# Ring tiles of 1024 columns loaded in four transfers (by field and by column half) in place of two (by field)

## The chip, the cores and the metric

The kernel runs on one core of a Trainium2 chip. The metric is the device time of one execution in microseconds (us), taken as the median of several runs. The engines of a core work in parallel and meet only at semaphores: TensorE (PE in the profile, PEld for its weight loads), VectorE (DVE), ScalarE (ACT), GpSimd (POOL), and SyncE (SP), which here does nothing but issue DMA transfers and wait for room. "SPq", "ACTq" and "POOLq" are the instructions of these engines that issue transfers or handle semaphores; they are not counted as busy.

## The reference

A recommendation model (xDeepFM) with a batch of 512, 39 fields and embeddings of 16 numbers:

```python
e = emb_table[feat_index]                       # 512 x 39 x 16
flat = e.reshape(512, -1)
linear_part = flat @ linear_w + linear_b
x0 = e
h1 = relu(einsum('bhd,bmd,ohm->bod', x0, x0, conv_w1) + conv_b1[None, :, None])   # 128 outputs
nxt, hi1 = split(h1, 2, axis=1)                 # 64 and 64
h2 = relu(einsum('bhd,bmd,ohm->bod', nxt, x0, conv_w2) + conv_b2[None, :, None])  # 128 outputs
res = concatenate([hi1, h2], axis=1).sum(axis=2)
y = relu(bn(flat @ deep_w1 + deep_b1, bn_g1, bn_b1))     # 400, batch norm over the batch
y = relu(bn(y @ deep_w2 + deep_b2, bn_g2, bn_b2))        # 400
out = concatenate([linear_part, res, y], axis=1) @ out_w + out_b
```

## The kernel before

The batch is cut into nine parts: parts 0 and 1 have 32 rows each, parts 2 to 8 have 64. One row of the batch gives 16 columns (one for each embedding number), so a tile of parts 0 and 1 has 512 columns and one of parts 2 to 8 has 1024; BANK is 512 columns, and CHUNKS_OF[j] says how many BANKs a tile of part j has (1 or 2).

GpSimd gathers the embeddings row by row, TensorE transposes them, ScalarE copies the result out and writes it to a scratch tensor in HBM, xs, laid out by part and field: for each field of a part one contiguous row of 512 or 1024 numbers of 4 bytes.

Layer 1 multiplies pairs of fields elementwise and contracts them with w1 ("x" tiles, six for each part; the multiplicand is put in place by TensorE at line 878, the product goes to placed). Layer 2 needs, for each pair of fields 2t and 2t+1, the product of the 64 rows nxt with field 2t (partitions 0 to 63) and with field 2t+1 (partitions 64 to 127): 20 tiles for each part. Most of these are "d" tiles: SP loads field 2t, repeated over 64 partitions, and field 2t+1, repeated over the other 64, into one of the eight slots of ring (a source with a partition step of zero); DVE multiplies the slot in place by p_n at line 732; TensorE contracts it with w2 at line 898. The few "p" tiles are put in place by TensorE instead of being loaded. Of the d tiles 38 have 512 columns and 129 have 1024.

The order of all tiles is one list written out by hand, SEQ; LOADED is the list of the d tiles in it, m the number of a tile in LOADED and m % 8 its slot. Each engine walks the same list. TensorE contracts a tile either in full precision (four matmul records for 1024 columns) or, for the tiles in SPLITS, as a high part (made by ScalarE, line 1095) and a low part (made by DVE at line 700 or by GpSimd at line 609), six records.

SP's program: the first loads of indices and weights; then for each m a wait until the slot's former tile has been used up (wait_used, its wait stands at line 372 in the profile), then the transfers of line 572. Behind the first d tile of part 3 (m = 55) stand load_flat for parts 0 and 1 and load_deep, 36 transfers of the deep layers' inputs and weights (lines 505 and 526 to 533), which TensorE needs from line 966 on. Every transfer raises the slot's semaphore s_load by 16, and DVE waits in product for the sum.

Of the kernel before, what the change touches and what calls it, by code (L numbers as in the profile page):

```python
# [6 lines left out]
BATCH, FIELDS, DIM, VOCAB = 512, 39, 16, 125000  # L7
H1, H2 = 128, 128
NEXT = H1 // 2
# [8 lines left out]
BANK = 512  # L18
# [11 lines left out]
TOK_OF = [DIM * r for r in ROWS_OF]  # L30
CHUNKS_OF = [t // BANK for t in TOK_OF]
# [102 lines left out]
RING, PLACED_RING, HIGH_RING, LOW_RING = 8, 4, 6, 7  # L134
# [33 lines left out]
SEQ, AT, WHERE = [], {}, []  # L168
# [13 lines left out]
LOADED = [s for s, tile in enumerate(SEQ) if tile[0] == 'd']  # L182
# [9 lines left out]
def rows_of(s):  # L192

    kind, _, t = SEQ[s]
    return X_ROWS[t] if kind == 'x' else 128
# [6 lines left out]
def build(nc, idx, emb, lin_w, lin_b, w1a, w1b, b1, w2, b2, dw1, db1, g1, be1, dw2, db2, g2, be2,  # L202
# [5 lines left out]
    xs = nc.dram_tensor("xs_scratch", [BLOCKS * FIELDS, TOK], F32).ap()  # L208

    def xs_at(b, field):  # L210

        return FIELDS * DIM * FROM[b] + field * TOK_OF[b]

    def xs_rows(b, field, n, stride):

        return bass.AP(xs.tensor, xs_at(b, field), [[stride * TOK_OF[b], n], [1, TOK_OF[b]]])

    ctx = ExitStack()
    with ctx:
        def sb(name, shape, dt=F32):  # L220
            return ctx.enter_context(nc.sbuf_tensor(name, shape, dt))
# [4 lines left out]
        def sem(name):  # L226
            return ctx.enter_context(nc.semaphore(name))
# [10 lines left out]
        ring = sb("ring", [128, RING, TOK])  # L238
# [93 lines left out]
        s_load = [sem(f"s_load{r}") for r in range(RING)]  # L332
# [36 lines left out]
        def own_wait(eng, semaphore, value):  # L369

            eng.wait_ge(semaphore, value)
            eng.sem_inc(s_past, 1)
# [67 lines left out]
        for b in range(1, PARTS):  # L440
            j, n = WHERE[LAST_X[b]]
# [40 lines left out]
        def scratch_write(eng, b, writes):  # L482

            for q, group, groups, fields in writes:

                r = ROWS_OF[b]
                dst = bass.AP(xs.tensor, xs_at(b, FLAT_FIELDS[b][0] * q + PER_GROUP[b] * group),
                              [[r, DIM * fields], [PER_GROUP[b] * TOK_OF[b], groups], [1, r]])
                src = xT[0:DIM * fields, q, r * group:r * (group + groups)].rearrange("p (g b) -> p g b", g=groups)
                eng.dma_start(dst, src).then_inc(s_xs, 16)  # L490

        def load_first_x(eng, b):
            eng.dma_start(xa[0:FIELDS, b % 2, 0:TOK_OF[b]], xs_rows(b, 0, FIELDS, 1)).then_inc(s_first_x, 16)

        def load_xa(eng, b):
            cols = slice(0, TOK_OF[b])
            for g in range(1, 3):
                eng.dma_start(xa[FIELDS * g:FIELDS * (g + 1), b % 2, cols], xs_rows(b, 0, FIELDS, 1)).then_inc(s_xa, 16)
            eng.dma_start(xa[3 * FIELDS:, b % 2, cols], xs_rows(b, 0, EXTRA, 1)).then_inc(s_xa, 16)
# [7 lines left out]
        def load_half_indices(eng, block, g):  # L507

            r, n = ROWS_OF[0], PER_GROUP[0]
            half, quarter = divmod(g, 2)  # L510
            src = idx[ROWS * half:ROWS * (half + 1), block, n * quarter:n * (quarter + 1)].rearrange("(c r) f -> r c f", c=2)
            eng.dma_start(idx_raw[r * g:r * (g + 1), block, :].rearrange("r (c f) -> r c f", c=2), src).then_inc(s_idx, 16)

        def load_w1(eng, dst, src):

            for t, p, n, (tile, row) in W1_RUNS:
                eng.dma_start(dst[p:p + n, t, :], src[row:row + n, tile, :]).then_inc(s_w, 16)  # L517


        @block.sync  # L520
        def _(sp):
            def load_deep():

                for c, p, first, fields in FLAT_PIECES:
                    row, r = DIM * first, DIM * fields
                    sp.dma_start(dw1_sb[p:p + r, c, 0:HIDDEN], dw1[row:row + r, :]).then_inc(s_small, 16)
                    sp.dma_start(dw1_sb[p:p + r, c, HIDDEN:], lin_w[row:row + r, :]).then_inc(s_small, 16)
                for n, v in enumerate((db1, g1, be1, db2, g2, be2)):
                    sp.dma_start(vec[:, n, :], v).then_inc(s_small, 16)
                for dst, src in ((lb_sb[HID_K:, :], lin_b), (ow_y_sb[HID_K:, HID_T - 1:], ow_lin),  # L530
                                 (ow_y_sb[0:HID_K, :], ow_y), (ow_h2_sb[:, :], ow_h2), (ob_sb[:, :], ob)):
                    sp.dma_start(dst, src).then_inc(s_small, 16)
                sp.dma_start(ow_hi_sb[NEXT:128, :], ow_hi).then_inc(s_small, 16)

            for g in range(2):
                load_half_indices(sp, 0, g)
            for block in range(1, HALVED):
                for g in range(2):
                    load_half_indices(sp, block, g)
            sp.dma_start(idx_raw[:, HALVED:, :], idx[:, HALVED:, :]).then_inc(s_idx, 16)  # L540
            for g in range(3):
                sp.dma_start(wq_whole[FIELDS * g:FIELDS * (g + 1), :], w1a[0:FIELDS, 6, :]).then_inc(s_w, 16)
            load_w1(sp, w1s, w1a)
            sp.dma_start(w2s[:, 0:L2_PAIRS, :], w2[0:128 * L2_PAIRS, :].rearrange("(t p) o -> p t o", p=128)).then_inc(s_w, 16)
            for half in range(2):
                sp.dma_start(w2s[NEXT * half:NEXT * (half + 1), TAIL, :], w2[128 * L2_PAIRS:, :]).then_inc(s_w, 16)  # L546
            sp.dma_start(b1_sb[:, :], b1).then_inc(s_bias, 16)
            for half in range(2):
                sp.dma_start(b1_dup[NEXT * half:NEXT * (half + 1), :], b1[0:NEXT, :]).then_inc(s_bias, 16)
            sp.dma_start(b2_sb[:, :], b2).then_inc(s_bias, 16)  # L550

            own_wait(sp, s_x, X_COPIED[0])
            scratch_write(sp, 0, XS_WRITES[0][1:])
            own_wait(sp, s_xs, XS_LANDED[0])
            sp.wait_ge(s_zero, 4)
            load_first_x(sp, 0)

            for m, s in enumerate(LOADED):
                _, j, t = SEQ[s]
                if s == L2_OF[j][0] or LOADED[m - 1] < L2_OF[j][0]:  # L560

                    own_wait(sp, s_xs, XS_LANDED[j])
                if m == 0:
                    own_wait(sp, s_sym, len(W1_SUMS))
                if m == FIRST_LOADS:
                    own_wait(sp, s_xs, XS_LANDED[1])
                    load_first_x(sp, 1)
                    load_xa(sp, 1)
                if m >= RING:
                    wait_used(sp, LOADED[m - RING])  # L570
                for half in range(2):
                    sp.dma_start(ring[NEXT * half:NEXT * (half + 1), m % RING, 0:TOK_OF[j]],  # L572
                                 xs_rows(j, min(2 * t + half, FIELDS - 1), NEXT, 0)).then_inc(s_load[m % RING], 16)
                if j == HALVES + 1 and LOADED[m - 1] < L2_OF[j][0]:
                    for b in range(HALVES):
                        load_flat(sp, b)
                    load_deep()


            sp.wait_ge(s_res, 1)  # L580
            sp.dma_start(out.rearrange("b o -> o b"), res[:, :]).then_inc(s_out, 16)
            sp.wait_ge(s_out, 16)
# [56 lines left out]
        def _(dve):  # L639
# [68 lines left out]
            def product(s):  # L708

                kind, b, t = SEQ[s]  # L710
                r = rows_of(s)
                if kind == 'd':
                    m = LOADED.index(s)
                    dve.wait_ge(s_load[m % RING], 32 * (m // RING + 1))
                    x = z_of(s)
                elif kind == 'p':
                    dve.wait_ge(s_copy, COPIED.index(s) + 1)
                    x = z_of(s)
                else:
                    a = PLACED.index(s)  # L720
                    if a >= PLACED_RING:
                        wait_used(dve, PLACED[a - PLACED_RING])
                    dve.wait_ge(s_place, a + 1)
                    x = (p_h2 if s < X_TILES and a % 2 else p_x)[0:r, 0:TOK_OF[b]]
                if kind == 'x':
                    dve.wait_ge(s_first_x, 16 * (b + 1))
                    dve.wait_ge(s_xa, XA_LANDED * (b + 1))
                    by = xa[0:r, b % 2, 0:TOK_OF[b]]
                else:
                    dve.wait_ge(s_n, b + 1)  # L730
                    by = p_n[b % 2][:, 0:TOK_OF[b]]
                nc.vector.tensor_tensor(z_of(s), by, x, ALU.mult).then_inc(s_z, 1)  # L732
# [512 lines left out]
```

## Time and profile before

| | |
|---|---|
| time before, median of 3 runs | 462.38 us (462.13 to 462.69) |
| the profiled execution: span of its instructions | 461.5 us |
| the profiled execution: time outside the span | not given by the page; the median of the runs is 0.9 us above the span |
| PE busy | 408.8 us (89% of the span) |
| DVE busy | 366.4 us (79%) |
| POOL busy | 296.7 us (64%) |
| ACT busy | 196.5 us (43%) |
| moved by DMA | 88.65 MB, mean 192 GB/s |

How to read it: busy is the time in which an engine had an instruction of its own at work. A line of groups gives the line of the kernel, the engine, the operation and its tiles, and how often it ran. "Idle before, releaser" is the time in which the engine stood still just before these instructions, and what ended most of it. A DMA issue has two times: how long the issuing engine is held by it, and how long after its start the data has landed.

### The profile page before, as it was taken

The numbers are of one execution on the slowest core, as the hardware profiler recorded it, in microseconds if no ns is written. First come the engines' busy times: TensorE is split into PE (matmuls) and PEld (weight loads), VectorE is DVE, ScalarE is ACT, GpSimd is POOL, SyncE is SP. The second block draws the span as 40 slices with busy tenths as digits, with TensorE's granted clock in tenths as the row PEclk, the third lists the DMA queues.
The fourth block names the chain that finished last, engine by engine and source line by source line (L and its number), as shares of the span: only waits on it lengthen the run. The fifth ranks groups of instructions, "written<-read, shape, count | busy, mean of one in ns | idle before, by whom it ended". The sixth has DMA issues, their size and how long they took to land.

```text
span 461.5 us, 4691 instructions
## 1 busy us (share of the span) xinstructions
PE 408.8 (89%) x1228; PEld 228.0 (49%) x1228; DVE 366.4 (79%) x406; ACT 196.5 (43%) x252; POOL 296.7 (64%) x221
## 2 busy tenths in 40 slices
PE   0027975999799999999999999999999999979996
PEld 0013432454355465555555556556557565654562
DVE  5252875587978889788989899997883998898894
ACT  1132316026323462365237524743563346574543
POOL 5787777477477258897689777861586247419472
PEclk9999899799999999999999999999999999999999
DMA  3853889659999979999799989999947996899770
GB/s 62 139 103 61 200 206 195 132 110 208 235 244 223 169 189 261 256 235 250 167 228 222 226 186 212 235 238 261 239 109 199 236 227 169 208 241 242 174 183 2
DMA packets 47515, 88.65 MB, mean 192 GB/s; under 512 B 18939, under 2 KB 24378, under 8 KB 47488
## 3 DMA queue, kind: packets, MB, share of 16 engines
q1 hardware_dynamic: 33545, 80.97, 72.2%
q0 software_dynamic: 5120, 1.32, 6.2%
q10 hardware_dynamic: 8823, 6.05, 6.1%
q8 instruction: 10, 0.16, 0.2%
q14 instruction: 17, 0.14, 0.1%
HBM read 87.03 MB, written 1.28 MB: 191 GB/s over the span
## 4 chain that ended last, share of the span: by engine, by line
PE 57%; POOL 10%; SPq 8%; DMA 8%; issue 7%; DVE 6%; ACT 2%; POOLq 1%; DVEq 0%; ACTq 0%
PE p_h L898 33%; PE p_n L898 12%; POOL G L595 8%; PE p_x L878 4%; DMA ring<-xs_scratch 4%; PE p_x L966 4%; PE p_n L966 3%; DVE ring L732 2%; POOL zl L609 2%; DMA G<-in_emb,idx_all 2%; SPq L517 2%; SPq L572 1%; SPq L505 1%; DMA w2s<-in_w 1%; SPq L546 1%
## 5 line engine op out<-in xcount | busy, mean ns | idle before, releaser
L595 POOL DMA_INDIRECT G<-in_emb,idx_all x160 | 167.9, 1050 | 49.3 <-issue 42.1
L732 DVE TENSOR_TENSOR ring<-p_n,ring 128x1024 f32<-128x1024 f32 (+1 forms) x167 | 177.7, 1094 | 16.6 <-DMA ring<-xs_scratch 9.6
L609 POOL TENSOR_TENSOR zl<-ring,zh 128x1024 fp32r<-128x1024 f32 (+1 forms) x52 | 121.1, 2341 | 108.0 <-ACT zh L1095 94.7
L898 PE MATMUL p_h<-ring,w2s 128*128 128x512 f32 x286 | 136.9, 606 | 5.2 <-DVE ring L732 4.5
L1095 ACT ACTIVATE zh<-ring 128x1024 fp32r<-128x1024 f32 (+1 forms) x79 | 80.7, 1029 | 139.5 <-DVE ring L732 137.1
L898 PE MATMUL p_n<-placed,w1s 125*128 125x512 f32 (+2 forms) x192 | 92.7, 604 | 0.0
L732 DVE TENSOR_TENSOR placed<-xa,p_x 125x1024 f32<-125x1024 f32 (+5 forms) x51 | 57.1, 1120 | 37.3 <-PE p_x L878 37.1
L898 PEld LDWEIGHTS p_h<-ring,w2s 128*128 128x128 f32 x286 | 55.0, 194 | 58.9 <-issue 47.5
L878 PE MATMUL p_x<-stack,put 103*125 103x512 f32 (+3 forms) x117 | 55.4, 547 | 13.8 <-DVE stack L705 12.2
L898 PE MATMUL p_h<-zh,w2l 128*128 128x512 f32 x169 | 65.4, 465 | 2.1 <-ACT h2s L1132 1.2
L898 PE MATMUL p_h<-zh,w2h 128*128 128x512 f32 x169 | 54.0, 398 | 0.0
L898 PEld LDWEIGHTS p_n<-placed,w1s 125*128 125x128 f32 (+2 forms) x192 | 37.1, 194 | 33.3 <-issue 29.6
L898 PE MATMUL p_h<-zl,w2h 128*128 128x512 f32 x153 | 49.5, 402 | 3.8 <-POOL zl L609 2.5
L898 PEld LDWEIGHTS p_h<-zh,w2l 128*128 128x128 f32 x169 | 31.7, 190 | 21.3 <-issue 10.8
L878 PEld LDWEIGHTS p_x<-stack,put 103*125 103x125 f32 (+3 forms) x117 | 22.0, 192 | 39.3 <-issue 27.9
L898 PEld LDWEIGHTS p_h<-zh,w2h 128*128 128x128 f32 x169 | 31.9, 189 | 8.0 <-issue 0.5
L898 PEld LDWEIGHTS p_h<-zl,w2h 128*128 128x128 f32 x153 | 28.5, 190 | 13.0 <-POOL zl L609 4.5
L700 DVE TENSOR_TENSOR zl<-ring,zh 128x1024 fp32r<-128x1024 f32 (+1 forms) x24 | 30.2, 1256 | 1.4 <-ACT zh L1095 1.3
L1111 ACT ACTIVATE placed<-p_x 128x1024 f32<-128x1024 f32 (+1 forms) x13 | 12.4, 957 | 34.8 <-PE p_x L878 34.7
L831 PE MATMUL p_x<-ident,G 128*128 128x128 f32 (+2 forms) x23 | 4.2, 289 | 24.2 <-DMA G<-in_emb,idx_all 23.3
L756 DVE TENSOR_REDUCE hi_sum<-hi 64x64 f32<-64x1024 f32 (+1 forms) x9 | 15.8, 1755 | 4.0 <-ACT hi L1103 4.0
L966 PE MATMUL p_x<-flatT,dw_sb 128*100 128x512 f32 (+3 forms) x40 | 17.8, 592 | 0.0
(107 smaller groups left out, 275.9 us busy)
## 6 DMA issues: line engine op xcount, KB each, us to landing
ring<-xs_scratch SPq DMA_DIRECT2D x258, 256.0 KB, 6.5
ring<-xs_scratch SPq DMA_DIRECT2D x76, 128.0 KB, 3.8
xa<-xs_scratch ACTq DMA_DIRECT2D x21, 156.0 KB
G<-in_emb,idx_all POOLq DMA_INDIRECT x160
xs_scratch<-xT ACTq DMA_DIRECT2D x16, 64.0 KB
dw_sb<-in_dw SPq DMA_DIRECT2D x4, 200.0 KB
xa<-in_dw ACTq DMA_DIRECT2D x2, 156.2 KB
xa<-xs_scratch SPq DMA_DIRECT2D x4, 78.0 KB
```

The lines of the kernel that those rows point to most:

```text
L505: eng.dma_start(flatT[p:p + DIM * fields, c, FROM[b]:FROM[b] + ROWS_OF[b]], src).then_inc(s_flat, 16)
L517: eng.dma_start(dst[p:p + n, t, :], src[row:row + n, tile, :]).then_inc(s_w, 16)
L595: nc.gpsimd.indirect_dma_start(G[:, b % 2, DIM * f:DIM * (f + 1)], None, emb[:, :], bass.IndirectOffsetOnAxis(index_of(b, f), 0)).then_inc ...
L609: nc.gpsimd.tensor_tensor(low_of(s), z_of(s), high_of(s).bitcast(F32), ALU.subtract).then_inc(s_low_pool, 1)
L700: nc.vector.tensor_tensor(low_of(s), z_of(s), high_of(s).bitcast(F32), ALU.subtract).then_inc(s_low_dve, 1)
L732: nc.vector.tensor_tensor(z_of(s), by, x, ALU.mult).then_inc(s_z, 1)
L756: return nc.vector.tensor_reduce(dst[:, FROM[b]:FROM[b] + ROWS_OF[b]], src[:, 0:TOK_OF[b]].rearrange("p (d b) -> p b d", d=DIM), AX.X, ALU ...
L878: last = nc.tensor.matmul(acc[0:rows_of(s), BANK * c:BANK * (c + 1)], put, stack[:, b % 3, BANK * c:BANK * (c + 1)], start=True, stop=True)
L898: return nc.tensor.matmul(acc[:, BANK * c:BANK * (c + 1)], w, x[:, BANK * c:BANK * (c + 1)], start=start, stop=stop)
L966: last = nc.tensor.matmul(p_d[0:end - HID_K * t, :], w[:, HID_K * t:end], x, start=c == 0, stop=c == len(parts) - 1)
L1095: nc.scalar.activation(high_of(s), z_of(s), ACT.Copy).then_inc(s_zh, 1)
L1111: nc.scalar.activation(z_of(s), p_x[:, 0:TOK_OF[SEQ[s][1]]], ACT.Copy).then_inc(s_copy, 1)
```

## The change

Each load of a d tile is written as a loop over CHUNKS_OF[j] column halves with the two fields inside. A tile of 1024 columns is loaded by four transfers of 64 partitions x 512 columns (128 KB) in place of two of 64 x 1024 (256 KB); the order is columns 0 to 511 of both fields, then columns 512 to 1023. A tile of 512 columns is loaded by two transfers as before. DVE waits, in product, for the sum of the increments of all tiles that its slot has had, 32 for each BANK. The slots, their order, the waits for room and everything on other queues stay as they are.

```diff
--- before.py
+++ after.py
@@ -568,9 +568,11 @@
                     load_xa(sp, 1)
                 if m >= RING:
                     wait_used(sp, LOADED[m - RING])
-                for half in range(2):
-                    sp.dma_start(ring[NEXT * half:NEXT * (half + 1), m % RING, 0:TOK_OF[j]],
-                                 xs_rows(j, min(2 * t + half, FIELDS - 1), NEXT, 0)).then_inc(s_load[m % RING], 16)
+                for c in range(CHUNKS_OF[j]):
+                    for half in range(2):
+                        src = bass.AP(xs.tensor, xs_at(j, min(2 * t + half, FIELDS - 1)) + BANK * c, [[0, NEXT], [1, BANK]])
+                        sp.dma_start(ring[NEXT * half:NEXT * (half + 1), m % RING, BANK * c:BANK * (c + 1)],
+                                     src).then_inc(s_load[m % RING], 16)
                 if j == HALVES + 1 and LOADED[m - 1] < L2_OF[j][0]:
                     for b in range(HALVES):
                         load_flat(sp, b)
@@ -711,7 +713,7 @@
                 r = rows_of(s)
                 if kind == 'd':
                     m = LOADED.index(s)
-                    dve.wait_ge(s_load[m % RING], 32 * (m // RING + 1))
+                    dve.wait_ge(s_load[m % RING], 32 * sum(CHUNKS_OF[SEQ[LOADED[q]][1]] for q in range(m % RING, m + 1, RING)))
                     x = z_of(s)
                 elif kind == 'p':
                     dve.wait_ge(s_copy, COPIED.index(s) + 1)
```

## Rows read from the trace of the kernel before

**Rows 1.** The page: engine table (busy us, share, instructions) and the chain that ended last.
```profile
PE 408.8 (89%) x1228; PEld 228.0 (49%) x1228; DVE 366.4 (79%) x406; ACT 196.5 (43%) x252; POOL 296.7 (64%) x221
...
PE p_h L898 33%; PE p_n L898 12%; POOL G L595 8%; PE p_x L878 4%; DMA ring<-xs_scratch 4%; PE p_x L966 4%; PE p_n L966 3%; DVE ring L732 2%; POOL zl L609 2%; DMA G<-in_emb,idx_all 2%; SPq L517 2%; SPq L572 1%; SPq L505 1%; DMA w2s<-in_w 1%;
```

**Rows 2.** Windows: length; PE, PEld, DVE, ACT, POOL busy us (count); PE clock, DMA share, GB/s.
```profile
206.00:387.00 181.00, 180.81 (x566) 104.96 (x565) 159.27 (x134) 86.26 (x102) 118.39 (x74) 1.00 0.91 213
387.00:442.00 55.00, 52.54 (x177) 31.92 (x177) 47.63 (x60) 31.18 (x36) 29.02 (x14) 1.00 0.90 213
```

**Rows 3.** The waits of the whole span: who waited for whom, us, times, longest.
```profile
DVE ring L732 <- DMA ring<-xs_scratch: 9.6, 10, 2.1
```

**Rows 4.** SP's waits and ring loads (line 572) in 106.3:443.1; KB and landing.
```profile
SPq L372 <- PE p_h L898: 127.1, 49, 10.2
...
SPq L372 <- DVE zh L695: 2.3, 2, 1.5
...
L572 SPq DMA_DIRECT2D ring<-xs_scratch x258: 444/588/1399, 106.3 to 442.5; - x129
...
ring<-xs_scratch SPq DMA_DIRECT2D x258, 256.0 KB, 6.5
```

**Rows 5.** SP's issues in order of time: start us, us, line, tiles, count.
```profile
145.50 6.54 SPq L505 DMA_DIRECT2D flatT<-xs_scratch  x12
...
162.31 0.47 SPq L533 DMA_DIRECT2D ow_hi_sb<-in_ow_hi  x1
162.90 7.56 SPq L572 DMA_DIRECT2D ring<-xs_scratch  x12
```

**Rows 6.** Line 572 in 46:52 and 50:64 (tiles of 512 columns): ns min/median/max.
```profile
L572 SPq DMA_DIRECT2D ring<-xs_scratch x10: 525/596/600, 45.7 to 51.4; - x10
...
DMA to landing us min/median/max: 3.2/3.3/3.3
...
DMA to landing us min/median/max: 3.5/3.8/4.1
```

**Rows 7.** SP's waits, line 572 (36 transfers) in 106.3:145.4.
```profile
SPq L372 <- PE p_h L898: 16.3, 8, 4.5
...
L572 SPq DMA_DIRECT2D ring<-xs_scratch x36: 444/588/752, 106.3 to 144.9; - x36
```

**Rows 8.** DVE's and PE's instructions in time: start us, us, what, idle before.
```profile
167.82 1.23 DVE L732 TENSOR_TENSOR ring<-p_n,ring 128x1024 f32<-128x1024 f32 x1 [1.26 <-DMA ring<-xs_scratch]
...
203.92 3.47 DVE L732 TENSOR_TENSOR ring<-p_n,ring 128x1024 f32<-128x1024 f32 x3
...
409.26 1.23 DVE L732 TENSOR_TENSOR ring<-p_n,ring 128x1024 f32<-128x1024 f32 x1
...
172.10 0.72 PE L898 MATMUL p_h<-zh,w2l 128*128 128x512 f32 x2
...
411.77 1.03 PE L898 MATMUL p_h<-zh,w2l 128*128 128x512 f32 x2
```

**Rows 9.** SP's waits and line 572 in 195.5:391.8.
```profile
SPq L372 <- PE p_h L898: 81.9, 33, 10.2
...
SPq L372 <- DVE zh L695: 1.5, 1, 1.5
...
L572 SPq DMA_DIRECT2D ring<-xs_scratch x149: 444/588/1399, 194.9 to 391.2; - x149
```

**Rows 10.** SP: wait just before 386.84, line 572 in 386.5:443.1; DVE's last product.
```profile
SPq L372 <- PE p_h L898: 7.3, 1, 7.3
...
L572 SPq DMA_DIRECT2D ring<-xs_scratch x50: 444/588/967, 386.8 to 442.5; - x50
...
452.34 1.22 DVE L732 TENSOR_TENSOR ring<-p_n,ring 128x1024 f32<-128x1024 f32 x1
```

**Rows 11.** SP's DMA queue: packets, MB, share of 16 engines; windows 46:68, then 350:366.
```profile
q1 hardware_dynamic: 2577, 4.23, 68.5%
...
q1 hardware_dynamic: 1136, 3.72, 100.1%
```

## The prediction

> **What bounds the kernel now.** I read the engine table first: TensorE (PE) is busy 408.8 of 461.5 us, and in the long middle, 206 to 387 us, 180.81 of 181 us [rows 1, 2]. So until the change opens holes in it, PE sets the time. The chain of work that ended last says the same: PE's lines 898, 878 and 966 hold 56% of it, and the ring's loads 4% (18 us) [rows 1]. Then who waits for the ring: VectorE (DVE), which turns each loaded tile into a product, stood idle for a load 10 times, 9.6 us in all [rows 3]. Transfers are near a limit too: the 16 DMA engines are 90 and 91% busy in the two late windows [rows 2].
>
> The queue that the change touches is SP's, and the page gives it no busy share, so I worked one out. In 106.3 to 443.1 us it issues all 258 transfers of 256 KB, and waits 158.7 us for room in the ring (four rows of 127.1 down to 2.3 us) [rows 4]. The other half of that stretch goes into issuing. The reader should see here how much SP time is left: 158.7 us.
>
> **What the change adds.** The 129 tiles of 1024 columns get four transfers each in place of two: 258 more issues on SP, no byte more. The 38 tiles of 512 columns (parts 0 and 1) keep their two transfers, so nothing moves before 106 us.
>
> *Price of one issue.* Twelve transfers back to back, six tiles with the semaphore step between them, span 7.56 us, 0.63 to 0.64 each [rows 5]. Is an issue cheaper when it carries half the bytes? Parts 0 and 1 are exactly that form (64 partitions, 128 KB): ten of them took 525 to 600 ns with a median of 596 [rows 6]. The bytes make no difference that these rows show. I take 0.60 us and 0.04 us of gap: 0.64. Bounds: 0.57 below (a 0.525 us issue and the gap), and, far off in shape, 0.55 (line 505, twelve issues in 6.54 us [rows 5]); 0.68 above, if slow issues, up to 1.4 us [rows 4], come more often. A full tile then costs SP 1.28 + 2 x 0.64 = 2.55 us (0.01 rounded off).
>
> *Sum over the stretch.* 258 x 0.64 = 165.1 us added, against 158.7 us of waiting. SP is short by 6 us even if it never waits again.
>
> *Landing.* Transfers of 128 KB landed 3.3 and 3.8 us (medians) after their issue began [rows 6], about 3.0 us after it ended; those of 256 KB take 6.5 [rows 4], since they queue behind each other. So part of the SP time comes back as shorter queues, and I count it: each step below compares landing with the start of the product that needs it.
>
> **Step 1, to 163 us.** Part 2 and the first tile of part 3 are 18 tiles: 36 x 0.64 = 23.0 us added, 16.3 us of waits to absorb them: 6.7 us short [rows 7]. Behind the first load of part 3 SP issues 36 small transfers of the deep layers, 145.5 to 162.8 us, and only then the next ring load at 162.90 [rows 5]. These 36 move 6.7 us too; their users are PE's matmuls of line 966, which the table D1 places in part 6, three parts on, so that costs nothing. The ring load moves to 169.6, its four issues end 2.45 us later (no semaphore step), at 172.05, it lands at 175.1. Its product began at 167.82, after an idle of 1.26 us put down to this very load [rows 8]. There is no slack to eat: DVE is 7.2 us late.
>
> PE takes that tile at 172.10, its product having ended at 169.05: a cover of 3.05 us. The thinnest cover that I found is a product ending at 410.49 and its matmul at 411.77, 1.28 us. So 1.8 us are eaten and PE is 5.4 us late at once; as thinner covers pass by, its lateness nears DVE's 7.2 [rows 8].
>
> **Step 2, to 387 us.** Fifteen more tiles of part 3 cost 15 x 2.55 = 38.3 us of SP; their products went from 167.82 to 206.2, 38.4 us [rows 8]: the lateness neither grows nor heals. From 195.5 to 391.8, 149 transfers add 95.4 us, and SP waited 104.4 us (four rows of 81.9 down to 1.5) [rows 9]: supply just keeps up. PE, busy 99.9%, has no idle in which to win time back [rows 2]. Between 5.4 and 7.2 I take 6.5 us of lateness for PE.
>
> **Step 3, the end.** At 386.84 SP issues after a wait of 7.3 us for PE; that room comes 6.5 us later, 393.3. From here 50 transfers, 25 tiles, remain: 25 x 2.55 = 63.8 us, last issue ends at 457.1, last landing 460.1. The last product starts at 452.34 [rows 10]. So DVE is 7.8 us late at the end, and the matmuls and sums behind it follow one by one. Beside that, some issues of before took up to 0.97 us there and up to 1.4 in the whole stretch [rows 4, 10]; where SP has no waits left these count in full, and there are twice as many issues: an estimate of 1.5 us more.
>
> Sum: 7.8 + 1.5 = 9.3 us. The profiled span of 461.5 becomes 470.8; the median of the runs, 462.38, is 0.9 us above the span: 471.7, and I say **472.0**.
>
> **Bounds of the sum.** At 0.57 per issue the addition falls to 147.1 us, 11.6 us under the waits. Step 1 is then 4.2 us short and ends its four issues 2.3 us later: landing 172.4, DVE 4.6 us late, PE 2.8 at once and 3.6 a little later, and the end adds nothing: 466.0. At 0.68 (the 0.64 with slow issues twice as common as before) it is 175.4 us, 16.7 over the waits. My 7.8 us at the end are also 6.4 us short, plus 7.6 us of waits that SP cannot use (its last issue ends at 457.1 in place of 443.1), less 6.2 us given back behind it: the last product began 9.2 us after that end, and can begin 3.0 us after it. With the same two terms 16.7 + 7.6 - 6.2 = 18.1 us: 480.5.
>
> **A rule against this.** Before the rivals, the rows: an issue holds SP for 0.60 us and its 128 KB need about 0.5 us of all 16 DMA engines (below), so issuing is not the smaller of the two. The Trainium skill, page "DMA: Bandwidth & Descriptors", section "Issuing engines are not separate DMA queues", holds that the sequencer's time to start a transfer is usually small relative to the transfer itself. This trace disagrees for 128 KB; by that rule the added issues would hide and the kernel would stay where it is, which is rival A.
>
> **Rival A, the added issues hide.** Mechanism: SP's own time overlaps its waits wherever it falls, ring slots filled ahead carry each burst. For it: 158.7 us of waits nearly equal what is added; eight slots of ring. Against: the deep layers' issues leave the ring empty at 163 us, where slack is zero. Time: 462.4, up to 463.3 if 1 us of step 1 remains. Chance 0.04.
>
> **Rival B, faster: short rows move cheaper.** In 46 to 68 us SP's queue moved 4.23 MB in 68.5% of 22 us, 3.56 us a MB; in 350 to 366 us 3.72 MB in all of 16 us, 4.30 us a MB [rows 11]. For a tile of 0.524 MB that is 1.87 against 2.26 us. If issues overlapped better in runs of four (under line 505's 0.55 us, four in about 1.9 us), tiles would come each 1.9 us, and DVE's waits for loads would go. What PE can gain is its idle in the late windows, 0.19 + 2.46 = 2.6 us [rows 2], and I give it 2.5. Time 459.9. The point from which it decides: an issue under 0.50 us. Against: the same form took 596 ns in half-size tiles. Chance 0.03.
>
> **Rival C, much slower: SP never catches up.** The four issues run at 0.68 us or more, as in the slow ones of up to 1.4 us; a tile costs SP 1.28 + 2 x 0.68 = 2.64 us, more than the 2.59 us in which tiles are used on average ((452.34 - 167.82) / 110 [rows 8, 10]), so the kernel runs at SP's pace from step 1 on. Against: twelve in a row kept 0.63 [rows 5]. Time 481 to 488. Chance 0.09.
>
> **Rival D, only the first hole.** Step 1 stays, but SP's 104.4 us of waits after it [rows 9] let the ring fill again and PE's few idles, 2.6 us, take up part of the lateness before the end, where the shorter landing leaves nothing late. Time 465 to 466.5 (461.5 + 5.4 us of step 1, less 1.3 to 2.6, plus 0.9). Chance 0.09.
>
> **How the numbers follow.** My forecast, SP-bound at 2.55 us a tile, lateness 4 to 17 us, has 0.75: time 472.0. The range 466 to 481 holds it and the lower edge of C; D's most part and A and B stay out. About 0.2% (0.9 us) is what a measurement here can tell from no change. Faster by over that: 0.03. Within: 0.04. Slower: 0.93.
>
> **What the next profile would show.** Step price: line 572 with 516 transfers of 128 KB in its own form beside the 76, median near 0.6 us. Step 1: the first ring load behind the deep layers' transfers starts near 169.6, its product near 175. Steps 2 and 3: SP's waits for room after 106 us fall from 158.7 to about 10 us or less, DVE's idle put down to ring loads grows from 9.6 to 20 us or more, PE's busy time stays near 409 while the span grows. Time from issue to landing falls to 3 to 4 us, and bytes a second fall in the late part with the DMA share well under 0.9. I am wrong if SP still waits over 50 us for room, if issues come under 0.5 us apart, or if the load behind the deep layers starts before 166.

## The result: 480.2 us against 462.5, and the profile after

The changed kernel takes 480.19 us (median of 4 runs, 479.34 to 482.57) against 462.53 of the kernel before (4 runs, 462.13 to 465.42): a ratio of 1.0376, 95% interval 1.0336 to 1.0417. The profiled execution took 479.34 us with a span of 477.5; before, the span was 461.5. So the profiles leave 16.0 us to be explained; by the medians it is 17.7, since the profiled run of after is the fastest of its four. Medians below are of all runs of a kernel, but ratios and their intervals leave out the runs that the timing puts in a slower state, so a ratio can differ from the quotient of two medians. A second chip gave the unaltered changed kernel 481.55 against 463.21, ratio 1.0405 (1.0334 to 1.0477).

The page of after: engine table, TensorE's granted clock in 40 slices, SP's DMA queue, and the chain that ended last.

```profile
span 477.5 us, 4949 instructions
PE 415.5 (87%) x1228; PEld 229.3 (48%) x1228; DVE 369.8 (77%) x406; ACT 196.7 (41%) x252; POOL 296.0 (62%) x221
...
PEclk9998897999997999999999999999999999999989
...
q1 hardware_dynamic: 54185, 80.99, 56.6%
...
PE 49%; SPq 27%; DMA 7%; issue 6%; DVE 4%; POOL 4%; ACT 2%; POOLq 1%; DVEq 0%; ACTq 0%
```

Against [rows 1], PE is 6.7 us longer busy. SP's issues now hold 27% of the chain; line 574 (the ring's loads, 572 before) held 1% of it and holds 20.2%.

Waits of after. First the whole span, then SP's own waits for room in 104.9 to 461.9 us and its ring loads in the same stretch (ns min/median/max, first and last start).

```profile
DVE ring L734 <- DMA ring<-xs_scratch: 27.7, 22, 4.5
...
SPq L372 <- PE p_h L900: 3.5, 6, 1.8
...
L574 SPq DMA_DIRECT2D ring<-xs_scratch x516: 444/597/1357, 104.9 to 461.4; - x172
```

The 158.7 us that SP waited for room [rows 4] are down to 3.5: the queue that had half its time to spare has none. DVE's idle for loads goes from 9.6 [rows 3] to 27.7 us.

Windows of after (length; PE, PEld, DVE, ACT, POOL busy with counts; PE clock, DMA share, GB/s):

```profile
206.00:387.00 181.00, 178.45 (x560) 103.90 (x561) 159.46 (x134) 87.98 (x104) 120.31 (x77) 1.00 0.76 214
387.00:442.00 55.00, 52.02 (x170) 30.27 (x169) 45.83 (x50) 31.65 (x35) 29.16 (x13) 1.00 0.64 206
```

The DMA share falls from 0.91 and 0.90 [rows 2] to 0.76 and 0.64 for much the same rate of bytes. The 16 engines have room; they aren't given work in time, as SP's rows show next.

SP's issues of after in order of time (start, length, line, tiles, count):

```profile
104.85 47.00 SPq L574 DMA_DIRECT2D ring<-xs_scratch  x72
151.89 6.17 SPq L505 DMA_DIRECT2D flatT<-xs_scratch  x12
...
168.11 0.47 SPq L533 DMA_DIRECT2D ow_hi_sb<-in_ow_hi  x1
168.69 293.25 SPq L574 DMA_DIRECT2D ring<-xs_scratch  x444
```

The last row tells the second half. From 168.69 to 461.94 SP does nothing but issue 444 transfers, 3.5 us of waits included: (293.25 - 3.5) / 444 = 0.653 us each, 2.61 us a tile.

DVE's products of after (start, length, and the idle before with what ended it):

```profile
136.82 1.23 DVE L734 TENSOR_TENSOR ring<-p_n,ring 128x1024 f32<-128x1024 f32 x1 [3.35 <-DMA ring<-xs_scratch]
...
173.69 1.23 DVE L734 TENSOR_TENSOR ring<-p_n,ring 128x1024 f32<-128x1024 f32 x1 [4.51 <-DMA ring<-xs_scratch]
180.77 1.22 DVE L734 TENSOR_TENSOR ring<-p_n,ring 128x1024 f32<-128x1024 f32 x1 [3.19 <-DMA ring<-xs_scratch]
201.51 1.23 DVE L734 TENSOR_TENSOR ring<-p_n,ring 128x1024 f32<-128x1024 f32 x1 [2.99 <-DMA ring<-xs_scratch]
...
214.77 3.47 DVE L734 TENSOR_TENSOR ring<-p_n,ring 128x1024 f32<-128x1024 f32 x3
...
451.37 1.22 DVE L734 TENSOR_TENSOR ring<-p_n,ring 128x1024 f32<-128x1024 f32 x1 [0.70 <-DMA ring<-xs_scratch]
...
453.44 2.15 DVE L785 TENSOR_SCALAR bn<-mv 100x4 f32<-100x4 f32 x1
...
468.39 1.22 DVE L734 TENSOR_TENSOR ring<-p_n,ring 128x1024 f32<-128x1024 f32 x1
```

Set against the same products of before, these rows give the lateness as it grows. At first the changed kernel is ahead: the last product of part 1, in front of every altered load, stood at 109.45 against 110.92 us. Counted from the first product of part 2 it loses 17.5 us up to the last product (353.9 us against 336.4). The product at 173.69 was at 167.82: 5.9 us. The group of three at 214.77 was at 203.92 [rows 8]: 10.85 us. From there to 390 us I find 10.9 on every product but a few: the lateness stands still, with PE busy 178.45 of 181 us. From 396 us on it grows once more, and the last product, 452.34 before [rows 10], starts at 468.39: 16.05 us. What follows it takes 9.1 us in both kernels.

### The profile page after: what moved, and what is told of

Read it like the earlier page. It is cut to its first block, busy times and chain, and to the rows that moved or that the text cites. A ratio compares the mean times of both kernels' runs of the same rounds, so it can differ in the third digit from the quotient of the medians.

```text
span 477.5 us, 4949 instructions
## 1 busy us (share of the span) xinstructions
PE 415.5 (87%) x1228; PEld 229.3 (48%) x1228; DVE 369.8 (77%) x406; ACT 196.7 (41%) x252; POOL 296.0 (62%) x221
## 4 chain that ended last, share of the span: by engine, by line
PE 49%; SPq 27%; DMA 7%; issue 6%; DVE 4%; POOL 4%; ACT 2%; POOLq 1%; DVEq 0%; ACTq 0%
PE p_h L900 28%; SPq L574 20%; PE p_n L900 12%; DMA ring<-xs_scratch 5%; PE p_x L880 4%; POOL G L597 3%; PE p_x L968 3%; SPq L517 2%; SPq L505 1%; DMA w2s<-in_w 1%; SPq L546 1%; DVE ring L734 1%; DVE placed L734 1%; POOL zl L611 1%; SPq L526 1%
## 5 line engine op out<-in xcount | busy, mean ns | idle before, releaser
L734 DVE TENSOR_TENSOR ring<-p_n,ring 128x1024 f32<-128x1024 f32 (+1 forms) x167 | 178.5, 1095 | 35.9 <-DMA ring<-xs_scratch 27.7
L900 PE MATMUL p_h<-ring,w2s 128*128 128x512 f32 x286 | 139.4, 616 | 6.7 <-DVE ring L734 5.9
L880 PE MATMUL p_x<-stack,put 103*125 103x512 f32 (+3 forms) x117 | 56.0, 553 | 12.6 <-DVE stack L707 10.3
L900 PE MATMUL p_h<-zl,w2h 128*128 128x512 f32 x153 | 51.1, 413 | 10.9 <-POOL zl L611 5.9
L900 PEld LDWEIGHTS p_h<-zh,w2l 128*128 128x128 f32 x169 | 32.0, 192 | 23.1 <-issue 10.3
L734 DVE TENSOR_TENSOR placed<-p_n,placed 128x1024 f32<-128x1024 f32 (+1 forms) x13 | 14.8, 1136 | 5.8 <-ACT placed L1113 5.8
```

The lines of the kernel that those rows point to most:

```text
L880: last = nc.tensor.matmul(acc[0:rows_of(s), BANK * c:BANK * (c + 1)], put, stack[:, b % 3, BANK * c:BANK * (c + 1)], start=True, stop=True)
L900: return nc.tensor.matmul(acc[:, BANK * c:BANK * (c + 1)], w, x[:, BANK * c:BANK * (c + 1)], start=start, stop=stop)
```

## The experiments

**My theory (T1)** was that SP's time for issuing is the bound: about 0.64 us for each transfer of 64 partitions, whatever it carries. Its rivals: the short rows (2 KB in place of 4 KB) move worse; the number of transfers or of landings is what costs, by whatever means; only the hole behind the deep layers' loads matters. The runs were made on four sets of kernels, each with its own runs of the kernel before. On the chip of the first eight, the stretch up to 200 us is some 40 us longer for every kernel, that of before too (505.0 and 502.57 us); there the ratios and the time from part 3 on are read, and times of before in an experiment's text are that chip's.

The edits are shown cut. The kernels that load every tile by two transfers are edits of the kernel before, the others are shown against the changed kernel, and DVE's wait counts what a slot really gets. "Tile" is one of 1024 columns; tiles of 512 are never altered.

**Three transfers.** The first field whole, the second by column halves.

```diff
+PIECES = {1: [(0, 0, 64, 0, 512), (1, 64, 64, 0, 512)],
+          2: [(0, 0, 64, 0, 1024), (1, 64, 64, 0, 512), (1, 64, 64, 512, 512)]}
...
+                for half, p0, n, c0, cols in PIECES[CHUNKS_OF[j]]:
+                    src = bass.AP(xs.tensor, xs_at(j, min(2 * t + half, FIELDS - 1)) + c0, [[0, n], [1, cols]])
+                    sp.dma_start(ring[p0:p0 + n, m % RING, c0:c0 + cols], src).then_inc(s_load[m % RING], 16)
```

> Three transfers for a tile of 1024 columns: the first field whole (64 partitions x 1024 columns, 256 KB), the second in two column halves. Theory 1 (SP's issue time is the bound, 0.64 us each): 129 x 0.64 = 82.6 us are added to SP where it waited 158.7 us, so it keeps about 75 us of waits, part 2 stays within its 16.3 us (18 x 0.64 = 11.5), and the time is 462 to 465. Theory 2 (rows of 2 KB fare badly on the DMA engines beside the 4 KB rows of the ACT queue, whatever SP does): half of the ring's bytes come in such rows, so about half of the loss, 470 to 472.

503.15 us (489.94 to 504.95) against 505.0, too scattered for an interval. SP waited 60.6 us for PE and 9.4 for POOL, so it has time left. From the product behind the deep layers' loads (the second of part 3) to the last it takes 285.2 us, against 284.5 (before) and 286.1 (the kernel with joined runs, below) with two transfers, and 293.7 to 296.4 in three kernels of the same chip that have four column pieces from part 3 on. Half of the added issues, no loss that shows. A cost per short row or per transfer should have shown half its size. This speaks for T1; the time as a whole has no ratio.

**Four transfers, cut by partitions.** As many transfers and as many bytes in each as in the change, but 32 partitions x 1024 columns: rows of 4 KB stay.

```diff
...
+          2: [(0, 0, 32, 0, 1024), (0, 32, 32, 0, 1024), (1, 64, 32, 0, 1024), (1, 96, 32, 0, 1024)]}
```

> Four transfers of 128 KB for a tile of 1024 columns, cut by partitions (32 x 1024 columns) and not by columns: rows of 4 KB as before, as many issues as after the change. Theory 1: if an issue of 32 partitions holds SP for the same 0.60 us, 475 to 482, SP's waits for room under 30 us. Theory 2: rows are as before, so 462 to 466.

493.25 against 505.0, ratio 0.9806 (0.9662 to 0.9949). On a quieter chip the same kernel again, beside the unaltered change:

> Four transfers by partitions (32 x 1024 columns) again, now beside the changed kernel on one chip. Its issues took 0.42 us in place of 0.60, so four cost 1.88 us a tile in place of 2.55. Theory 1: SP keeps about 60 us of waits, and it is within 0.98 to 1.00 of the kernel before, 3 to 5% under the changed kernel, although both issue 516 transfers of 128 KB. Rival (the number of transfers costs, not SP's time): near the changed kernel.

> The changed kernel once more, unaltered, beside the kernel before on the chip of the other experiments, whose first 200 us are longer for every kernel. Theory 1 (SP's issue time plus the holes that it opens): 1.030 to 1.045 of the kernel before here too. If it were under 1.02, the loss would hang on the other chip.

462.86 against 463.21, ratio 0.9997 (0.9971 to 1.0023), where the change has 1.0405. So the 0.98 of the first chip isn't a gain. The page and SP's rows of the kernel cut by partitions:

```profile
PE 409.4 (89%) x1228; PEld 227.6 (49%) x1228; DVE 368.1 (80%) x406; ACT 196.6 (43%) x252; POOL 295.6 (64%) x221
...
L575 SPq DMA_DIRECT2D ring<-xs_scratch x516: 302/421/1680, 106.2 to 444.4; - x172
...
SPq L374 <- PE p_h L900: 65.7, 28, 9.4
SPq L374 <- POOL zl L611: 9.9, 8, 2.4
```

The same of the change in that set of runs (the last row: SP in 105 to 450 us):

```profile
PE 416.2 (87%) x1228; PEld 229.3 (48%) x1228; DVE 369.0 (77%) x406; ACT 196.9 (41%) x252; POOL 296.0 (62%) x221
...
SPq L372 <- PE p_h L900: 3.6, 6, 2.0
```

This pair settles the first question. Both kernels issue 516 transfers of 128 KB for these tiles and wait on as many landings. One pays 0.42 us for each and has 75.6 us of SP time over; the other pays 0.60 and has 3.6. The number of transfers costs nothing that shows; what differs with SP's time for them is 4%. It leaves the row size open, since the two differ in that too.

**Row size alone.** Two transfers a tile, each row in two runs of 512 numbers. The first try wrote the two runs next to each other:

```diff
+                    src = bass.AP(xs.tensor, xs_at(j, min(2 * t + half, FIELDS - 1)), [[0, NEXT], [BANK, CHUNKS_OF[j]], [1, BANK]])
+                    sp.dma_start(ring[NEXT * half:NEXT * (half + 1), m % RING, 0:TOK_OF[j]].rearrange("p (c k) -> p c k", k=BANK),
```

> Two transfers for a tile of 1024 columns as before, with both access patterns written as two runs of 512 columns, so that rows of 2 KB are moved by two issues, if the runs are kept apart (the packet sizes of the trace show it; if they are joined the kernel is the one before, 462.5). Theory 1: SP has its waits back, 459 to 464, a little faster where transfers bind. Theory 2: near the changed kernel, 475 to 481.

504.93 against 505.0 (ratio 0.9906 to 1.0246), and the trace still has 47515 packets, those of before: neighbouring runs were joined, and already in the program, since the issued instructions of the trace have elements of 4096 bytes. The run says nothing on rows. With a gap of 8 numbers between the halves in the ring they stay apart:

```diff
+GAP = 8
...
-        ring = sb("ring", [128, RING, TOK])
+        ring = sb("ring", [128, RING, CHUNKS, BANK + GAP])
...
+                    sp.dma_start(ring[NEXT * half:NEXT * (half + 1), m % RING, 0:CHUNKS_OF[j], 0:BANK], src).then_inc(s_load[m % RING], 16)
```

> Two transfers for a tile as before, but a slot of the ring has a gap of 8 numbers between its column halves, so that each row must be moved as two runs of 2 KB (packets of 2048 bytes in the trace). It tells the short rows from the issues. Theory 1: SP's issues stay near 0.6 us each, its waits stay near 150 us, and the time is 0.99 to 1.00 of the kernel before; DMA share in the late windows falls as in the changed kernel. Rival (short rows lose their turn beside the ACT queue's long rows, and that makes the holes): 1.015 or more.

465.79 against 463.21, ratio 1.0066 (1.0029 to 1.0103), over the 0.99 to 1.00 that I had expected. The profile is of a run of 468.91 us. Its packets, SP's ring loads (count, KB, landing), SP's waits in 105 to 450 us, and the window that [rows 2] shows of before:

```profile
DMA packets 64027, 88.65 MB, mean 190 GB/s; under 512 B 18939, under 2 KB 24378, under 8 KB 64000
...
ring<-xs_scratch SPq DMA_DIRECT2D x258, 256.0 KB, 7.6
...
SPq L373 <- PE p_h L907: 120.2, 48, 9.0
...
206.00:387.00 181.00, 179.87 (x566) 105.05 (x565) 159.42 (x131) 85.45 (x101) 113.96 (x72) 1.00 0.99 212
```

The ring's rows of full tiles are all short now and SP has its waits. This kernel is 0.7% slower, and the DMA share rises from 0.91 to 0.99, where I had expected it to fall. So short rows aren't cheaper but, if anything, dearer while transfers queue behind each other (the edit also changes how the engines address the ring; DVE's products took 1.095 us on the mean against 1.094). In the change, whose DMA share is 0.76 there, the engines aren't near full; the part of its 4% that is due to rows can't be more than this 0.7% (1.0% at the upper end of the interval) unless the two work on each other, and that wasn't tried apart.

**Five transfers.** The last quarter of the tile cut once more (64 KB pieces).

```diff
...
+          2: [(0, 0, 64, 0, 512), (1, 64, 64, 0, 512), (0, 0, 64, 512, 512), (1, 64, 64, 512, 256), (1, 64, 64, 768, 256)]}
```

> Five transfers for a tile of 1024 columns: as the change, with the last quarter-megabyte-half cut once more (64 x 256 columns twice). Theory 1: SP has no waits left, so each further issue counts in full: 129 x 0.64 = 82.6 us on top of 480, 555 to 565. Theory 2: only an eighth of the bytes has shorter rows than in the changed kernel, 481 to 488.

597.91 against 505.0, ratio 1.1902 (1.1747 to 1.2057). As a ratio T1's 555 to 565 was 1.20 to 1.22; the interval reaches into that, and the rival's 1.04 to 1.06 is far off. Its waits for loads, its chain and SP's issues behind part 3's first tile, up to 570 us:

```profile
DVE ring L734 <- DMA ring<-xs_scratch: 119.0, 68, 15.7
...
SPq 67%; issue 13%; another core or an unknown queue 7%; PE 5%; DVE 4%; ACT 2%; DMA 1%; POOLq 0%; ACTq 0%; DVEq 0%
...
223.73 346.51 SPq L575 DMA_DIRECT2D ring<-xs_scratch  x531
```

The price again is 346.51 / 531 = 0.653 us, with pieces of 64 and 128 KB mixed and no wait between. One issue more in each of the 111 tiles behind part 3's first should add 111 x 0.65 = 72 us; from the first product of part 3 to the last it took 377.1 us against 301.7 in the change, 75.4 more. (From part 2 on it is 441.0 against 353.9, but there this chip's long stretch comes in.) That is the size and the place that T1 gives, and the clearest of its numbers. The third and fourth transfer together had cost 16.0 us, the fifth alone some 75: a cost for each landing or each byte has no reason to grow so, a queue that has run out of waits has.

**Where in time.** Part 2 with two transfers a tile, four from part 3 on:

```diff
+SPLIT_OF = [1 if j <= 2 else CHUNKS_OF[j] for j in range(PARTS)]
...
-                for c in range(CHUNKS_OF[j]):
+                for c in range(SPLIT_OF[j]):
```

> Four transfers for a tile only from part 3 on; part 2 keeps two. Theory 1 (SP's issue time): part 2 no longer runs SP short ahead of the deep layers' transfers, so the hole at 137 us, the stretch of TensorE at 1.2 GHz behind it and the late load at 174 us go; from 163 us on SP adds 112 x 1.28 = 143.4 us to 142.4 us of waits. Ratio to the kernel before 1.013 to 1.028 (469 to 475 on a chip that gives 462.5). Rival (the loss is made by the late parts alone, where the products wait from 390 us on): as the changed kernel, 1.035 to 1.040.

511.53 against 502.57, ratio 1.0183 (1.0084 to 1.0282): inside what was expected. DVE's waits for loads are 10.8 us. It is slower than before though step 1 of the prediction is undone, so the first hole isn't the whole cause.

**The deep layers' loads out of the way.** The 24 transfers of load_deep are issued early, at the wait of the fourth load, in the change:

```diff
                 if m == FIRST_LOADS:
+                    load_deep()
                     own_wait(sp, s_xs, XS_LANDED[1])
...
-                    load_deep()
```

> The changed kernel with the 24 transfers of load_deep (10.8 us of SP) moved from behind the first load of part 3 to SP's wait of 11.3 us ahead of the fourth load. Theory 1: the load behind the deep layers comes some 10 us earlier, its product waits no more, and SP's shortage as a whole shrinks by 10.8 us: ratio 1.013 to 1.025 (469 to 474). Rival (landing times beside the ACT queue's transfers make the holes, not SP): 1.033 to 1.040.

> The changed kernel with load_deep moved early, again, since its first runs (about 1.027) fell on the chip whose first 200 us are long. Theory 1: 10.8 us of SP's work leave the stretch in which SP has no waits, so the ratio falls from 1.0405 to 1.015 to 1.028 and VectorE's wait for the first load behind the deep layers (4.5 us and more) is gone. Rival: what is taken off SP there is lost again beside the ACT queue's transfers, 1.033 to 1.040.

On the first chip 516.32 against 502.57, 4 scattered runs and no interval; repeated elsewhere 472.79 against 462.44, ratio 1.022 (1.0184 to 1.0255), inside what was expected. Its rows:

```profile
PE 412.8 (87%) x1228; PEld 227.9 (48%) x1228; DVE 370.3 (78%) x406; ACT 196.9 (42%) x252; POOL 295.3 (63%) x221
...
168.44 1.22 DVE L734 TENSOR_TENSOR ring<-p_n,ring 128x1024 f32<-128x1024 f32 x1
...
159.91 296.34 SPq L575 DMA_DIRECT2D ring<-xs_scratch  x444
```

The load behind the deep layers starts 8.8 us earlier, its product has no wait in front, and the last issue ends at 456.25, 5.7 us earlier. Some 10.5 us of other issues (158.1 to 168.6 in the change) taken off SP's full stretch bought back 7.4 us on the medians, 480.19 to 472.79, on two chips; by the ratios, 1.0376 to 1.022, it is 7.2. In the profiles it is 5.6 us, and nearly all of it stands already at the product behind the deep layers' loads, 168.44 against 173.69; from there to the last product both take the same (294.4 and 294.7 us). No transfer of the ring was touched, so it isn't the ring's traffic that was made cheaper; what moved is 24 issues and the deep layers' bytes.

The same move in the kernel before, where SP has time to spare:

> The kernel before with the same move of load_deep. SP had 158.7 us of waits left, so its time is worth nothing but at the load behind the deep layers (1.26 + 0.78 us of idle of VectorE): theory 1 says 0.997 to 1.000 of the kernel before, that is 461 to 462.5; over 1.003 would say that the megabyte moved early is in the way of the first parts' loads.

504.07 against 502.57, ratio 1.0095 (1.0022 to 1.0167). I had expected no change (0.997 to 1.000). The 24 transfers now stand in front of early loads, and the last product of part 0 came at 88.2 us; in the kernel with the joined runs, which is that of before, it came at 83.5, but in the changed kernel with the same move only at 84.5 on this chip, and at 71.1 against 68.1 on two others. So the move isn't free even there, how much it costs isn't settled, and it gains nothing where SP isn't short: the gain in the change is the queue's.

**Short rows on ACT's queue too.** Looking for why landing took 6 to 7 us at a few places, I cut ACT's loads of xa by column halves as well.

```diff
...
+            for c in range(CHUNKS_OF[b]):
+                cols = slice(BANK * c, BANK * (c + 1))
+                for g in range(1, 3):
+                    eng.dma_start(xa[FIELDS * g:FIELDS * (g + 1), b % 2, cols], xs_cols(b, FIELDS, c)).then_inc(s_xa, 16)
...
```

> The changed kernel with the loads of xa on the ACT queue (4 KB rows) cut into column halves as well, so that both queues move rows of 2 KB. Theory of the landing (a queue of 4 KB rows takes twice the bytes of a queue of 2 KB rows while both have work): the ring's loads that landed 6 to 7 us after their issue in 127 to 139 us and 192 to 200 us land in under 5, VectorE's idle for ring loads falls from 27.7 us by 4 to 8, ratio 1.025 to 1.033 (474 to 478). Theory that only the bytes count: 1.036 to 1.040, landing as before.

530.96 (523.34 to 533.8) against 502.57, some 5.6%, far over what I had expected, without an interval. The excess over the change isn't in the ring: from part 3's first product to the last this kernel takes 300.2 us, the change 301.7. It lies early. Between the last product of part 0 (84.52) and the next (105.56) stand 21.0 us, in which ScalarE waits 24.1 us for something that the profile puts down to a remote cause; the kernel with joined runs has the same 21 us in its profile (83.50 to 104.71), the six other kernels of this chip have 6.0 to 7.5. Whether the edit brings that stretch on isn't shown. DVE's waits for loads are 17.2 us against 27.7 in the change on another chip, but 18.6 in the changed kernel with the deep loads early on this one, and the product of tile 48 in LOADED still began 5.7 us after the tile's issues had ended. The idea that long rows on one queue crowd out short ones on another got no support that can be told from the chip's own scatter.

## Why the prediction was right, and where its size came out wrong

The sign and the mechanism were right: SP's issue time eats its waits, opens a hole behind the deep layers' loads and sets the pace of the end. The range held 480.2, at its upper end, and that was partly luck. Its bound of 480.5 stood for 0.68 us an issue. At the 0.653 that was measured the prediction's own sum gives 258 x 0.653 = 168.5, less 158.7, plus 7.6, less 6.2: 11.2 us, or 473.6. The rest came from a wrongly chosen tile and from a DVE instruction that no bound held, and the second chip's 481.55 lies outside the range. The size was wrong: 9.3 us of lateness were forecast and 16.0 came.

**What the profile confirmed.** The issue of 128 KB: median 0.597 us against 0.60. SP's waits: 3.5 us against "about 10 or less". DVE's idle: 27.7 against "20 or more". Step 1: the load behind the deep layers started at 168.69 (forecast 169.6), its product at 173.69 (forecast "near 175"), with 4.51 us of idle in front of it. DMA share 0.64 to 0.76, "well under 0.9". The bytes made no difference to the issue, as the two sizes of before had said. Landing, "3 to 4 us" from the issue, came to 3.1 us for the load behind the deep layers and 2.8 at 449 us, but to 7.7 and 6.9 at two places below.

**A page's rule.** The pair of kernels with 516 transfers each shows that SP's issue time, added 258 times, decides. The Trainium skill, page "DMA: Bandwidth & Descriptors", section "Issuing engines are not separate DMA queues", calls the sequencer's time usually small beside the transfer's. At 64 partitions these runs don't agree where transfers follow each other: 0.597 us for an issue whose bytes need about 0.5 us of the 16 engines (an estimate from [rows 11]). Beside one transfer's whole time to its landing, 2.8 us and more, the issue is the smaller.

**Where 6.7 us were lost.** The end can be followed tile by tile. From the last five tiles of after,

```profile
L574 SPq DMA_DIRECT2D ring<-xs_scratch x20: 524/596/597, 449.3 to 461.4; - x20
```

the sixth tile from the end has its issues done at 449.2 us. It landed 2.2 us later, and its product at 451.37 is the last that waited for a load. In the kernel before it is the third of these:

```profile
434.61 3.49 DVE L732 TENSOR_TENSOR ring<-p_n,ring 128x1024 f32<-128x1024 f32 x3
...
438.95 0.59 DVE L783 TENSOR_SCALAR bn<-mv 100x4 f32<-100x4 f32 x1
```

It began there at 434.61 + 3.49 - 1.22 = 436.88, so it is 14.5 us late. Everything behind it follows in the same steps but one: line 785 (783 before) took 2.15 us in place of 0.59, 1.56 more. 14.49 + 1.56 = 16.05. My 9.3 us and these 16.05 differ by four terms:

1. *The wrong tile, 2.7 us.* This is the step that failed. Step 3 compared the last landing with the last product. But before, five tiles from the end a product ran much closer to SP: its start was 436.88. My own numbers gave 457.1 - 5 x 2.55 + 3.0 = 447.4 for that tile, 10.5 us late, not 7.8. The tiles at the end aren't used at an even pace (DVE has the deep layers' sums in between), so the comparison had to be made for each of them.
2. *The price of an issue, 3.3 us.* 0.653 us on the mean, not 0.64, over 444 issues: 5.8 us, and 1 us more or less from the waits and the start. SP's last issue ended at 461.9, 4.8 us after the forecast 457.1. I had set 1.5 aside for slow issues. A median of 0.60 with gaps hides them; a long stretch without waits shows the mean. It fell well short of the 0.68 of my upper bound.
3. *Landing, -0.8 us.* 2.2 us after the issue's end at this place, not 3.0.
4. *Line 785, 1.56 us.* It took 1.70 to 2.15 us in all six profiles with four column pieces up to the end, 0.57 to 0.59 in those with two, three, or four cut by partitions, and 0.17 with five. The traces say what it waits for. GpSimd's instructions beside it, after (two, back to back), then before:

```profile
450.80 4.77 POOL L611 TENSOR_TENSOR zl<-ring,zh 128x1024 fp32r<-128x1024 f32 x2 [0.86 <-ACT zh L1097]
...
437.10 2.41 POOL L609 TENSOR_TENSOR zl<-ring,zh 128x1024 fp32r<-128x1024 f32 x1 [0.85 <-ACT zh L1095]
```

They end at 455.57 and 439.51, and DVE's instruction, begun at 453.44 and 438.95, ends 0.02 to 0.03 us later, at 455.59 and 439.54. The same holds in all 13 profiles in which a 2.4 us instruction of GpSimd was running; with five transfers none was, and it took 0.17 us. So its length is what was left of GpSimd's instruction when DVE came to it, 0.59 us before and 2.15 after: a chance of phase that follows from the shifted products, and no step of mine had it.

7.8 + 2.7 + 4.8 - 0.8 + 1.56 = 16.06, of which 9.3 were forecast.

**Step 2 was wrong on the way, though not for the end.** "The lateness neither grows nor heals" to 387 us. It stood from 217 us on, but at 10.9 in place of 7.2. Two assumptions failed before that. The ring ran dry already at 136.82, with 3.35 us of idle, 37 us ahead of step 1's hole; and landing isn't always 3.0 us behind the issue. From the chain of waits of after:

```profile
132.85 7.66 DMA ring<-xs_scratch
196.92 6.86 DMA ring<-xs_scratch
```

At 132.85 and 196.92 a ring load in the chain took 7.7 and 6.9 us. Around the first of them the 16 engines were shared with ACT's loads of xa (132 to 138 us, MB and share by queue):

```profile
q1 hardware_dynamic: 364, 0.60, 43.6%
q10 hardware_dynamic: 169, 0.51, 35.9%
```

SP's queue moved 0.60 MB in 6 us, 100 GB/s; its four issues a tile had offered some 200. Before, the load of the same tile had been issued at 122.8 us, not 127.8, and landed at 133.1, 3.4 us ahead of its use: the lead covered the slow landing, and the change took the lead away. The second place looks alike: in 194 to 203 us ACT's queue moved 0.50 MB at a share of 21.1%. That the sharing is what delays the landings wasn't tested.

**PE's busy time was forecast to stay near 409 and came to 415.5.** The granted clock is at its lower level for longer. Windows of after at a granted clock of 0.50, which is 1.2 GHz in place of 2.4, then those of before:

```profile
142.80:149.60 6.80, 6.65 (x14) 4.49 (x15) 5.57 (x6) 2.06 (x3) 5.58 (x5) 0.50 1.07 226
460.20:463.60 3.40, 3.40 (x5) 1.39 (x5) 3.29 (x5) 2.78 (x4) 0.31 (x1) 0.50 0.66 196
43.80:50.60 6.80, 5.83 (x9) 3.12 (x10) 5.82 (x9) 3.04 (x6) 4.98 (x6) 0.50 0.70 188
77.90:84.70 6.80, 5.51 (x8) 2.17 (x7) 4.57 (x5) 3.47 (x4) 5.28 (x6) 0.50 0.56 114
```

```profile
46.00:49.40 3.40, 3.40 (x6) 1.69 (x6) 3.27 (x6) 2.93 (x5) 2.50 (x3) 0.50 0.78 203
80.10:87.00 6.90, 5.96 (x8) 2.84 (x9) 3.64 (x4) 0.64 (x1) 5.18 (x6) 0.51 0.53 89
```

The windows at 1.2 GHz sum to 23.8 us in place of 10.3, and PE was busy 21.4 us in them in place of 9.4; half of the 12.0 more is 6.0 of the 6.7 us by which its busy time grew. Two of the four windows (43.8 and 77.9 us) lie ahead of every altered load and hold 1.0 of the 6.0; the other two stand behind holes. In front of the first window PE was busy 8.52 of 10.8 us, in front of the second it had stood idle for 1.45 us. The repetition on the other chip has such stretches behind its holes near 142, 177, 207 and 466 us; the kernel cut by partitions, without the holes, has none behind 88 us while PE works. It would be wrong, though, to book 6.7 us of the 16.0 on the clock. The chain at the end runs through SP, which waited for PE 3.5 us in all, and behind the last awaited load each step but line 785 takes what it took before. The slow clock at 460 us cost the end nothing. Behind the holes it came with them, off the path here; whether it has a share in the lateness of 2.6 us at 165 us wasn't tested.

**The rivals.** A (the issues hide) fell with the 3.5 us of waits. B (short rows cheaper) fell with 1.0066 for short rows alone. Its 3.56 us a MB [rows 11] doesn't go by row size: over the whole span SP's queue took 4.39 us a MB with short rows in two transfers, 4.12 before with long ones, and 3.34 in the change, whose rows are short too but whose transfers don't queue. C (SP never catches up) asked for 0.68 us and gives 481 to 488; the kernel stands between it and my forecast, with 0.653 us, the lateness growing at 130 to 206 and from 396 us on, and level in the middle. D (only the first hole) fell with the run that has two transfers in part 2 and still loses 1.8%.

## What to carry to other kernels

Splitting a transfer adds an issue at the price of the new form, and halving the columns didn't lower that price: before a split, take the issuing queue's waits over the stretch and compare them with the added issues at their mean from a long row without waits, not at the median. Here four transfers cut by partitions (0.42 us each) were free and four cut by columns (0.65 us with gaps) cost 4%. And when a queue loses its lead, look for the tile whose slack is least, near the end above all, and for the places where the lead had covered a crowded stretch of the DMA engines.

## What the runs showed of the hardware that I had not expected

- An issue's price doesn't go by bytes, nor by partitions alone. For the ring's loads 64 partitions took 0.597 us (median) with rows of 4, 2 or 1 KB alike (0.588 to 0.597), and 32 partitions 0.421. But lines 526 and 527 in SP's rows took 0.43 with 128 partitions, 0.48 and 0.60 with 64, 0.58 and 0.42 with 48. Which feature of a transfer sets its price stays open: it has to be measured for each form.
- With rows of 2 KB in place of 4 KB and transfers that queue, the DMA share was 0.99 against 0.91 in the same window, and the time 0.7% longer.
- A short VectorE instruction (line 785, 100 x 4 numbers) lasted until GpSimd's running instruction ended, in 13 of 13 profiles where there was one: 0.57 to 2.15 us in place of 0.17.
